# P.V in four 32-column tiles, row sums by other means, and a new PSUM layout in two attention layers

## The reference

```
# layer 0: self-attention with gates
p      = softmax(inner @ outer.T / sqrt(32))
attn   = p * aperture[q] * expression[k]           # both sigmoids, one value per head and position
attn   = attn / (attn.sum(-1) + 1e-8)
out    = (attn @ v, rotated and scaled per head) @ Wout
# layer 1: cross-attention, keys masked (mask 4 x 1024 x 1024 of 0/1)
p      = softmax(where(mask, q @ k.T / sqrt(32), -inf));  out = (p @ v) @ Wo + bo
# layer 2: 16 experts, a mixture of projections and one head of width 64 (unchanged)
```

## Time and profile before

| | us |
|---|---|
| runs | 5066.39, 5076.81, 5081.88; median 5076.81 |
| profiled execution, first to last instruction | 5068.7 |
| TensorE matmul busy | 4480.0 (88%), 19080 instructions |
| VectorE busy | 2950.8 (58%) |
| ScalarE busy | 1400.0 (28%) |
| GpSimd busy | 734.8 (14%) |
| mean granted TensorE clock | 0.944 of full speed |

### The profile page before, as it was taken

The page is one execution under the profiler, slowest core; times in us unless marked ns, Lnnn a source line. Parts: engine busy times, 40 slices in busy tenths (PEclk is TensorE's granted clock), DMA queues, the critical chain, the costliest instruction groups (busy, mean ns, idle before and its releaser), DMA issues. The chain is left out here.

```text
span 5068.7 us, 60158 instructions
## 1 busy us (share of the span) xinstructions
PE 4480.0 (88%) x19080; PEld 2464.3 (49%) x19080; DVE 2950.8 (58%) x5751; ACT 1400.0 (28%) x1693; POOL 734.8 (14%) x488
## 2 busy tenths in 40 slices
PE   6898899789988977999799979997999598989897
PEld 4334533543363335333543354335433276767676
DVE  3674476367546743664466546653665475757575
ACT  1333234223413421333133312341233302020202
POOL 2102210320021013102210131003100100000000
PEclk9999999899999988999899989998999798999998
DMA  2212211221122214210421042114211300000000
GB/s 81 59 39 73 65 38 51 69 57 38 38 80 59 55 45 139 51 38 26 162 59 37 27 154 57 37 38 144 65 38 30 125 11 33 18 33 19 34 17 17
DMA packets 114496, 285.92 MB, mean 56 GB/s; under 512 B 16240, under 2 KB 18160, under 8 KB 114160
## 3 DMA queue, kind: packets, MB, share of 16 engines
q1 hardware_dynamic: 87648, 213.54, 16.1%
q10 hardware_dynamic: 26512, 68.16, 3.9%
HBM read 137.48 MB, written 42.99 MB: 36 GB/s over the span
## 5 line engine op out<-in xcount | busy, mean ns | idle before, releaser
L781 ACT ACTIVATE probs<-scores 128x1024 f32<-128x1024 f32 x1024 | 1027.3, 1023 | 1637.0 <-PE scores L562 880.0
L580 PE MATMUL acc<-probs,v_ext 128*34 128x512 f32 x4096 | 1064.0, 606 | 1.0 <-DVE u L859 1.0
L627 PE MATMUL work<-stack 96*128 96x512 f32 x1792 | 876.8, 497 | 91.4 <-DVE q_raw L1033 31.2
L973 DVE CUSTOM_DVE_ANT_0 work<-work,mask_q 128x512 f32<-128x512 f32 x896 | 619.8, 704 | 327.9 <-PE work L627 305.2
L557 PE MATMUL scores<-stack 97*128 97x512 f32 x2048 | 785.3, 458 | 4.0 <-ACT probs L781 2.6
L977 DVE TENSOR_REDUCE mx<-work 128x1 f32<-128x512 f32 x896 | 602.8, 689 | 267.1 <-PE work L627 256.0
L627 PEld LDWEIGHTS work<-stack 96*128 96x128 f32 x1792 | 336.9, 190 | 820.3 <-issue 381.2
L518 PE MATMUL work<-stack,w 128*128 128x512 f32 x1536 | 382.7, 411 | 172.8 <-DVEq L871 152.1
L1336 PE MATMUL work_e<-w_in_e,x_e 128*128 128x512 f32 x2304 | 523.4, 389 | 0.0
L1336 PEld LDWEIGHTS work_e<-w_in_e,x_e 128*128 128x128 f32 x2304 | 432.2, 188 | 89.8
L557 PEld LDWEIGHTS scores<-stack 97*128 97x128 f32 x2048 | 396.0, 195 | 102.1 <-ACT probs L781 51.2
(11 more groups left out here) (228 smaller groups left out, 3974.6 us busy)
## 6 DMA issues: line engine op xcount, KB each, us to landing
stack<-qk SPq DMA_DIRECT2D x384, 256.0 KB, 4.9
stage<-x_t SPq DMA_DIRECT2D x32, 512.0 KB, 3.5
k_raw<-x SPq DMA_DIRECT2D x8, 2048.0 KB, 8.6
x_t<-xts ACTq DMA_DIRECT2D x16, 1024.0 KB, 6.8
x<-k_raw ACTq DMA_DIRECT2D x8, 2048.0 KB, 8.2
mstage<-mask ACTq DMA_DIRECT2D x32, 512.0 KB, 3.8
mstage<-mask_t ACTq DMA_DIRECT2D x32, 512.0 KB, 3.5
kv_raw<-ctx_t SPq DMA_DIRECT2D x4, 2048.0 KB, 7.9
```

The costliest lines, as they stand in the source:

```text
L580: last = pe.matmul(acc[64 * h:64 * h + VW, c, :], v_ext[:, kt, 2 * p + h, :], probs[:, n % PRING, c * CH:(c + 1) * CH], start=(kt == 0), s ...
L627: last = pe.matmul(bank[:, :], stack[0:3 * DH, s, h, t * P:(t + 1) * P], stack[0:3 * DH, s, 2 + h, c * CH:(c + 1) * CH], start=True, stop= ...
L781: act.activation(probs[:, n % PRING, :], scores[n % 2][:, :], ACT.Exp, scale=SCALE).then_inc(p_full, 1)
L973: dve.tensor_tensor_reduce(bank[:, :], bank[:, :], mask_q[:, t, c * CH:(c + 1) * CH], 1.0, -3e38, ALU.add, ALU.max, mx[:, p % 2, j:j + 1]) ...
```

## The change

- **P.V.** `v_ext` becomes `v` with 32 columns a head. The four products of a key tile (two heads, two query halves) go to the four 32-partition quadrants of one bank, `acc[32j:32j+32, 0, :]`, in one `pv` step in place of two.
- **Row sums, unmasked layer.** Four more matmuls a key tile with a 2-column stationary operand `e_one` (expression, 1) into `acc[32j:32j+2, 1, :]`. Then `sel`: two 128-column matmuls of 512 columns that spread the two sums over each quadrant, and VectorE computes `1/(sum_e + 1e-8 * sum_1 / aperture)` on 128x512; `1/aperture` goes out to DRAM and comes back as broadcasts, four DMAs a pair.
- **Row sums, masked layer.** For key tiles outside `direct_tiles(p)` (3 and 7; 3 to 7 in the last pair) GpSimd adds `probs` into `psums`, 128x1024 for each head (`add_tile`). For the direct ones TensorE multiplies `probs` with a 32-column block of ones into `acc[:, 1, :]`; a `sums` step does the same with `psums`, once a pair. VectorE clamps, takes the reciprocal of 128x512 and multiplies.
- **PSUM.** `wides` 2x2 banks for the maxima, now 1024 columns at a time (`sm`), and for `mneg`, `sel`, `RZ`; `halfs` 2x1 banks for `st`, now 512 columns at a time, and for the projections; `acc` 2 banks.
- **Order.** In a key tile: `st` of head 0, two `sm`, `st` of head 1, `pv` of the tile before. `den` and `bc` are gone. The rows without any valid key are handled in `out` instead of in the last pair.

Core of the diff:

```diff
-    GAPS = 4
+            steps += [("st", p, kt, 0, c) for c in range(NC_)]
+            rate = (0 if kt == 0 else 3) if p == 0 else 2      # sm steps
+            ...
+            steps += [("st", p, kt, 1, c) for c in range(NC_)]
+            steps += misc                                     # mneg when due
+            if not masked and p > 0 and kt == 2:
+                steps.append(("sel", p - 1))
+            if before[0] >= 0:
+                steps.append(("pv", *before))
+            if masked and p > 0 and kt == 1:
+                steps.append(("sums", p - 1))
...
-        work = [psum(f"work{b}", [P, CH]) for b in range(2)]
-        scores = [psum(f"scores{b}", [P, S]) for b in range(2)]
-        acc = psum("acc", [P, NC_, CH])
+        wides = [psum(f"wide{b}", [P, S]) for b in range(2)]
+        halfs = [psum(f"half{b}", [P, CH]) for b in range(2)]
+        acc = psum("acc", [P, 2, CH])
...
+                def add_tile(p, kt):                          # GpSimd
+                    m = pool_tiles[p].index(kt)
+                    for h in range(2):
+                        ...
+                        slot = kt % 2 * 2 + h
+                        if m == 0:
+                            pool.wait_ge(sums_taken, 1 + i * PAIRS + p)
+                            pool.tensor_scalar(psums[:, h, :], probs[:, slot, :], 1.0, 0.0, ALU.mult, ALU.add)
+                        else:
+                            pool.drain()
+                            pool.tensor_tensor(psums[:, h, :], psums[:, h, :], probs[:, slot, :], ALU.add)
...
-                        for h in range(2):                    # TensorE, pv
-                            last = pe.matmul(acc[64 * h:64 * h + VW, c, :], v_ext[:, kt, 2 * p + h, :],
-                                             probs[:, n % PRING, c * CH:(c + 1) * CH], ...)
+                        for c in range(NC_):
+                            for h in range(2):
+                                j = 2 * c + h
+                                last = pe.matmul(acc[DH * j:DH * (j + 1), 0, :], v[:, kt, 2 * p + h, :],
+                                                 probs[:, kt % 2 * 2 + h, c * CH:(c + 1) * CH], ...)
+                        if masked and kt in direct_tiles(p):
+                            ...                               # the same with ones[:, :] into acc[:, 1, :]
+                        elif not masked:
+                            ...                               # the same with e_one into acc[DH*j:DH*j+2, 1, :]
...
-                        act.activation(probs[:, n % PRING, :], scores[n % 2][:, :], ACT.Exp, scale=SCALE)
+                        if c == 0 and n >= 2:                 # n = p * TT + kt
+                            if h == 0:
+                                act.wait_ge(pv_done, 1 + i * PAIRS * TT + n - 1)
+                            if masked and (n - 2) % TT in pool_tiles[(n - 2) // TT]:
+                                act.wait_ge(added, ...)
+                        act.activation(probs[:, kt % 2 * 2 + h, c * CH:(c + 1) * CH], bank[:, :], ACT.Exp, scale=SCALE)
...
+                    elif kind == "sums":                      # VectorE, masked
+                        dve.tensor_scalar(u[:, 1, :], acc[:, 1, :], 1e-30, None, ALU.max).then_inc(sums_taken, 1)
+                        dve.reciprocal(u[:, 1, :], u[:, 1, :])
+                        normalise(p, u[:, 1, :])              # two tensor_tensor of 64x512, both inputs in SBUF
+                    elif kind == "sel":                       # VectorE, unmasked
+                        dve.scalar_tensor_tensor(out=den, in0=bank[:, CH:S], scalar=1e-8, in1=over_a[:, p % 2, :], ...)
+                        dve.tensor_tensor(den, bank[:, 0:CH], den, ALU.add)
+                        dve.reciprocal(den, den)
+                        normalise(p, den)
+                    elif kind == "out":
+                        if masked:
+                            dve.scalar_tensor_tensor(out=y[:, t, :], in0=rz, scalar=none[:, t:t + 1], in1=y[:, t, :], ...)
```

More of the change, by code:

```diff
@@ L15 @@
 PAIRS = H // 2
-VW = DH + 2
 EPS = 1e-5
@@ L46, in attention_steps @@
     rest += [("V", t) for t in range(TT)]
-    first = [("smax0", h, t) for h in range(2) for t in range(TT)]
+    first = smax(0)
     lead = 6
@@ L56, in attention_steps @@
             first = first[every:]
+    assert not first
     if masked:
         steps.append(("CS",))
-    GAPS = 4
     ahead = [m for p in range(1, PAIRS) for m in smax(p)]
-    left = 0
     due = []
     for p in range(PAIRS):
[L65 to L72, removed]
@@ new lines, in attention_steps @@
+            misc = due
+            due = []
+            rate = (0 if kt == 0 else 3) if p == 0 else 2
+            for _ in range(rate):
+                if ahead:
+                    m = ahead.pop(0)
+                    steps.append(m)
+                    if m[2:] == (1, TT - 1):
+                        due.append(("mneg", m[1]))
+            steps += [("st", p, kt, 1, c) for c in range(NC_)]
+            steps += misc
+            if masked and p == 2 and kt == 4:
+                steps.append(("RZ",))
@@ L94, in attention_steps @@
+            if not masked and p > 0 and kt == 2:
[4 more added lines that the diff above has]
+                steps.append(("sums", p - 1))
     assert not ahead and not due
-    steps += [("pv", PAIRS - 1, TT - 1, c) for c in range(NC_)]
-    steps += [(kind, PAIRS - 1, c) for kind in ("den", "bc") for c in range(NC_)]
+    steps.append(("pv", PAIRS - 1, TT - 1))
+    steps.append(("sums" if masked else "sel", PAIRS - 1))
@@ L97, in attention_steps @@
     steps += [("out", t) for t in range(TT)]
     steps += [("xt", t) for t in range(TT)]
-    if sum(s[0] not in ("st", "pv", "smax0") for s in steps) % 2:
-        steps.append(("pad",))
-    return steps
+    for kinds, name in ((WIDE_KINDS, "wpad"), (HALF_KINDS, "xpad")):
+        if sum(s[0] in kinds for s in steps) % 2:
+            steps.append((name,))
+    return steps
+WIDE_KINDS = ("sm", "mneg", "sel", "RZ", "wpad")
+HALF_KINDS = ("Q", "K", "EX", "AP", "V", "CS", "st", "out", "xt", "xpad")
@@ L385, in _ @@
                 stack_pair(2)
+                if not masked:
+                    spread_aperture(0)
                 max_row(1)
@@ L481, in _ @@
                     split_chunk(n)
-                for g in range(2, KT):
-                    split_group(g)
                 if masked:
+                    for p in range(PAIRS):
+                        for kt in pool_tiles[p]:
+                            add_tile(p, kt)
+                            if kt == 2 and p in (1, 3):
+                                split_group(p // 2 + 2)
                     pool.wait_ge(const_in, 16 * 6)
@@ L490, in _ @@
                     pool.engine_nop().then_inc(bo_added, 1)
+                else:
+                    for g in range(2, KT):
+                        split_group(g)
                 for t in range(TT):
@@ new lines, in _ @@
+                    if kind == "sums":
+                        p = step[1]
+                        pe.wait_ge(added, 1 + i * ADDS + sum(adds_of[:p + 1]))
+                        for c in range(NC_):
+                            for h in range(2):
+                                j = 2 * c + h
+                                last = pe.matmul(acc[DH * j:DH * (j + 1), 1, :], ones[:, :],
+                                                 psums[:, h, c * CH:(c + 1) * CH], start=False, stop=True,
+                                                 skip_group_check=True)
+                        last.then_inc(sums_done, 1)
+                        continue
@@ L586, in _ @@
-                    n = use_no[step]
-                    bank = work[n % 2]
-                    pe.wait_ge(work_free[n % 2], 1 + i * PER + n // 2)
-                    if kind in ("Q", "K"):
+                        last = pe.matmul(bank[:, :],
+                                         stack[0:3 * DH + 1, s, 2 + h, kt * P:(kt + 1) * P],
+                                         stack[0:3 * DH + 1, s, h, c * CH:(c + 1) * CH],
+                                         start=True, stop=not masked)
@@ L590, in _ @@
+                        if masked:
+                            last = pe.matmul(bank[:, :], eye8[:, :], mask_k[:, kt, c * CH:(c + 1) * CH],
+                                             start=False, stop=True)
+                    elif kind in ("Q", "K"):
                         _, g, c = step
```

483 lines of the change are left out of this document (243 added, 240 removed).

## The result

The changed kernel took 5138.3 us (median of 4 runs, 5134.7 to 5154.8), the kernel before 5071.6 (4 runs): a ratio of 1.0135, interval 1.0111 to 1.0159. It is 67 us slower; 27 faster was forecast (5045 against the 5071.6 of all four runs of before). The profiled span went from 5068.7 to 5136.9.

What follows compares the result with a forecast made beforehand. TensorE was taken to bound the pairs. Unmasked batches -6 us and masked -26 take the span from 5068.7 to 5037; adding 8.1 for the median of the runs gives 5045, range 4925 to 5200 for 8 in 10.

Steps and rivals of the forecast that it cites:

- Rival D: P.V and sums on TensorE: column tiles run only two at a time, eight MATMULs 1.70 us; chance .1.
- the unmasked end and last pair: Unmasked batch: pair 7 +8.2 us (33.0 against 24.8), end of the batch +3.2 us (9.2 against 5.97).
- the masked ones: Masked batch: pair 7 +5.7 us, `out` +5 as a mean, end of the last pair +.5.
- the cause given for the last pair: Scores in two 512-column banks, without `sm` between, make head 1 wait: +.93 us a key tile unmasked, +.6 masked.
- The burst is .7 + 3.4 + 1.6 + 1.35 = 7.1: VectorE in a masked pair: clamp, reciprocal, and two products, the first waiting for GpSimd's add; 7.1 us.
- Stalls 1.0 + 3.6 = 4.6: Masked pair: exponential of key tile 2 waits 1.0 us, `sm` of key tile 3 2.7 and .9; bounds 0 and 7.0.
- pair 39.6: Masked pair: 31.8 + 1.7 direct tiles + .85 `sums` + .65 `mneg` + 4.6 stalls = 39.6 us.
- rival C: Masked layer: GpSimd wins the port between the products (+67), `out` longer (+20), or tiles not quite fourfold; 5130 to 5200; chance .2.
- the -20.7: Masked pairs 1 to 6 of a batch: pairs 1 to 5 -18.1 us, pair 6 -2.6 us.
- +4.3 each in pairs 1 and 3 for GpSimd's splits: Masked pairs 1 and 3: exponentials from key tile 6 on wait for `split_group`, queued between GpSimd's adds; 4.3 us a time.
- masked pair 0, "+3": Masked pair 0: the copy key tile 2 needs is queued behind GpSimd's weight splitting, 15.6 us into the pair; +3 us.
- B, the hidden burst: All pairs: VectorE's burst hides, TensorE alone sets them; about 210 us off in all, half gives 4940; chance .2.

Runs made afterwards that it cites:

- the run with fillers: Twelve score matmuls with overwritten results added in key tile 3 of masked pairs 1 to 7, against the changed kernel: 5123.0 us, ratio 1.0099 to the kernel before.
- four small follow-ups: On the split-burst kernel: wide-bank last pair, bias adds and keyless rows in pair 7, more TensorE-summed tiles in masked pair 0, then in pairs 1 and 3: 4887.1 us.

## Why the prediction was wrong

**Right.** Four column tiles run at once: the first group of four MATMULs started at 2240.135 to 2240.155, the second at 2240.589 to 2240.609. Rival D is out. The Trainium skill's 2.38 for three column tiles ("TensorE: Matmul & The Clock Gate", Part 3: Packing small matmuls) doesn't carry over to these tiles: by the prediction's .43 a pass, eight one after the other are 3.4 us, and here they take .99 to the next start with the change of width in it (2240.14 to 2241.13) and .88 without (905.97 to 906.85), 3.5 to 3.9 times as fast. The unmasked pair (36.9, measured 37.2), the reciprocal (3.34, measured 3.35), the unmasked end and last pair (+11.4, measured +10.7) and the masked ones (+11.2, measured +10.8) held. So did the cause given for the last pair: with wide banks it went. An unmasked key tile takes 4.03, not 3.91.

**Wrong: "The burst is .7 + 3.4 + 1.6 + 1.35 = 7.1", "Stalls 1.0 + 3.6 = 4.6", pair 39.6.** This is the step that failed. Two things are missing in it. One was a stated bound and rival C: GpSimd gets the next add in between the two products, so they take 4.56 and not 2.95, +1.6 a pair. I had taken the value below the bound with no row for it; TensorE waits 5.8 us in pair 4 (5.0 for maxima, .8 for exponentials), not 4.6. The other was put at nothing without a word: where TensorE has stood 4.2 us it goes on at half clock, in all 24 masked pairs from 1 to 6, at least 6.8 us a pair, and at .37 to .45 us per us that is 2.5 to 3.1. With both, 39.6 + 1.6 + 2.8 = 44.0; measured 44.4 in pair 4 of the first batch and 43.2 in the three others. In the kernel before, pairs 1 to 6 had no half clock, with waits of up to 1.8 us unmasked and .7 masked; only pair 0 had some, 10.2 us in the unmasked layer, begun inside a wait of 7.0, and no row of the prediction looked at it. A stall that a change adds must be priced with the slow time behind it. Over a batch that takes the -20.7 to -4.5, some 65 us in all. The run with the reciprocal in PSUM gives 246.7 a batch for pairs 1 to 6, against a forecast of 247.7. That is partly luck: 17 to 24 us at half clock are in it, worth some 6 to 11 by the same slopes, which no term of the forecast has, so errors of about that size cancel, such as the next one.

**Wrong, smaller: +4.3 each in pairs 1 and 3 for GpSimd's splits.** They hardly added: 44.1 and 44.2 beside 44.4 in pair 4 of the first batch and 43.2 in the others. The stall had already made room for GpSimd. When the burst was split, these pairs stood at 42.5 or 42.8 beside 36.7, and the splits' price showed (5.8 with its half clock); two tiles less to add took 4 of it away. A cost can hide under the stall that one is about to remove.

**Wrong: masked pair 0, "+3".** It was +9.4. GpSimd ends its weights at 2053.2, 15 us into the pair, as forecast; ScalarE then stands 7.7 us for the copy of `psums` and TensorE 4.1 behind it, again with 9 to 13 us at half clock in the pair, where it had 2 to 4 before; at .4 us per us that difference is some 3 of the 9.4, an estimate. Tiles on TensorE gave back 4.3, with 3 to 5 us at half clock left. In unmasked pair 0 (+3, forecast 1.5) half clock went from 10.2 to 13.7 us, which by the slope of .45 is about the 1.5 that the forecast lacks. What the rest is was not tried.

**Rivals.** C's mechanism is what happened, in place and sign: port lost between the products, total 5130 to 5200. That its 5130 lies within 10 us of the 5138.3 is partly luck: it has 67 us for the products, which measure 1.6 a pair or 45 in 28 pairs, and nothing for the clock. The Trainium skill ("SBUF — State Buffer", SBUF: two separate sides) has the loser blocked for the whole instruction; the trace agrees for both products, of which each ends some .55 us after the add that it met (2241.85 and 2242.39, 2244.60 and 2245.15), a little less than one takes alone (.69). The run with one PSUM input shows that it is the second SBUF input that makes VectorE wait. B, the hidden burst, was not this kernel, but it is what splitting the burst makes of it: the unmasked pair of 35.1 is near the 34.8 given for it.

## What to carry to other kernels

When work leaves the engine that bounds a loop, list the longest uninterrupted run of instructions on each engine that feeds it and compare that with what the buffers between them cover: here two banks of 1024 columns could not cover 8.8 us of reciprocal and products, though VectorE was idle 14 of 44 us. Cut such a burst into pieces the size of the slack before judging the change; the change lost 1.3%, with the burst cut it won 2.5%, and with four small follow-ups, of which one (the bias adds in pair 7) did harm by its waits, 3.6%. Price a new stall of TensorE with the half-clock time behind it, and keep two-input SBUF operations of VectorE away from GpSimd's adds, or put one input in PSUM.

## What the runs showed of the hardware

- Four column tiles of 32, fp32 probabilities against fp32 values, 512 columns: four MATMULs within 20 ns of one another, the next four .45 us later.
- GpSimd's next add can start ahead of a VectorE product that is issued right behind another: products of 1.81 and 2.74 us in place of .68 to .72, each ending .55 us behind an add. With one input in PSUM, 1.39 for both, beside an add.
- After a stall of 4.2 us TensorE ran at 1.2 GHz for 6.8 us or more in each of 24 pairs. The longest wait is not all that decides: with 1.5 or 1.6 us in all masked pairs of the run with fillers, 6 had no half clock and 18 had 3.4 to 6.8 us; the kernel before kept its clock through waits of 1.8. One us at half clock cost .37 to .45 us of time in this mix, an estimate from differences between batches.
- VectorE's reciprocal of 512 columns takes 3.35 us on 128 partitions and 3.34 on 32; of 128 columns it takes .95.
